# A software-pipelined four-layer attention kernel: another order of the steps on every engine, with other lags and other PSUM banks

## The reference

```python
# L0: causal self-attention, cross-attention on ctx (16 heads of 16), feed-forward
x1 = layernorm(x + mha(x, x, Wq1, Wk1, Wv1, causal=True))
x2 = layernorm(x1 + mha(x1, ctx, Wq2, Wk2, Wv2))
x3 = layernorm(x2 + relu(x2 @ fc1.T + b1) @ fc2.T + b2)
#     in mha: lengths = sum(energy[:, :, 0, :] != 0); columns beyond are masked
# L1: attention of norm(x3) on norm(ctx), a 4-wide gelu MLP, a second attention
att = softmax(normF @ normX.T / 16) @ normX
cross = gelu(att @ w1.T) @ w2.T
nc = layernorm(cross);  x4 = normF + g2 * (cross + g1 * attention(nc, nc, nc))
# L2: x5 = x4 + softmax(x4 @ ctx.T) @ ctx
# L3: 8-head attention on norm(ctx), then a state space scan, then a modulation
x6 = x5 + mha8(layernorm(x5), layernorm(ctx)) @ Wo.T
u = (layernorm(x6) @ W_in.T) @ Bmat
s_t = silu(s_{t-1} @ A.T) + u_t;   out = x6 + s @ Cmat + mod
```

## Time and profile before

| | |
|---|---|
| median of 3 runs | 4112.46 us (4112.36 to 4113.29) |
| profiled execution, span | 4106.6 us (a run's time has 5.9 us more around it) |
| PE busy | 3913.2 us, 95% |
| ACT busy | 3547.9 us, 86% |
| DVE busy | 3349.2 us, 82% |
| POOL busy | 2854.5 us, 70% |

### The profile page before, as it was taken

One profiled execution on the slowest core, in us unless ns is written; L12 is line 12 of the kernel. 1 busy time (PEld: TensorE's weight loads), 2 busy tenths in 40 slices (PEclk: granted clock), 3 DMA queues, 4 the chain that ended last, 5 costly groups with the idle time before them and its releaser, 6 DMA issues. The chain is left out here.

```text
span 4106.6 us, 111739 instructions
## 1 busy us (share of the span) xinstructions
PE 3913.2 (95%) x37177; PEld 3233.6 (79%) x37177; DVE 3349.2 (82%) x9519; ACT 3547.9 (86%) x8460; POOL 2854.5 (70%) x3172
## 2 busy tenths in 40 slices
PE   6899999999999999999999999999999999999859
PEld 5688888888888888888888888888888888887647
DVE  4788888888888888888888888888888888888635
ACT  4799999999998999999899999989999998999635
POOL 2577777777777777777777777777777777777636
PEclk7999999999999999999999999999999999999969
DMA  3001011011101101110110111011011101100038
GB/s 115 22 29 34 20 31 34 20 34 31 34 20 31 34 21 33 31 34 20 31 34 23 31 31 34 20 31 34 23 32 31 34 20 31 34 24 28 18 80 306
DMA packets 121876, 159.94 MB, mean 39 GB/s; under 512 B 12296, under 2 KB 108450, under 8 KB 116642
## 3 DMA queue, kind: packets, MB, share of 16 engines
q1 hardware_dynamic: 116896, 145.39, 11.5%
q10 hardware_dynamic: 4416, 7.41, 0.5%
HBM read 114.86 MB, written 37.75 MB: 37 GB/s over the span
## 5 line engine op out<-in xcount | busy, mean ns | idle before, releaser
L618 PE MATMUL bank<-ident,prob 128*128 128x128 f32 x5120 | 728.8, 277 | 56.9 <-ACT CR L1005 26.9
L938 ACT ACTIVATE probT<-bank 128x512 f32<-128x512 f32 x1280 | 730.6, 593 | 59.6 <-PE bank L618 56.7
L909 ACT ACTIVATE turned<-bank 128x512 f32<-128x512 f32 x896 | 538.7, 601 | 186.9 <-PE bank L554 177.8
L618 PEld LDWEIGHTS bank<-ident,prob 128*128 128x128 f32 x5120 | 590.9, 142 | 138.4 <-issue 48.8
L1138 DVE TENSOR_REDUCE mx<-bank 128x4 f32<-128x512 f32 x768 | 507.9, 682 | 187.3 <-PE bank L589 184.7
L927 ACT ACTIVATE prob<-prob,mx 128x128 f32<-128x128 f32 x2048 | 650.6, 396 | 4.1 <-DVE mx L1127 4.0
L562 PE MATMUL bank<-turned,shared 128*128 128x256 f32 x2560 | 616.4, 384 | 1.2 <-ACT turned L909 1.1
L1444 POOL TENSOR_TENSOR rs_ln<-ve_ln,half 128x2 f32<-128x2 f32 x320 | 227.3, 710 | 446.8 <-DVE ve_ln L1109 446.8
L1149 DVE TENSOR_TENSOR prob<-bank,mx 128x512 f32<-128x512 f32 x768 | 520.7, 685 | 15.3 <-PE bank L618 1.9
L562 PEld LDWEIGHTS bank<-turned,shared 128*128 128x128 f32 x2560 | 469.8, 191 | 69.0 <-issue 12.3
L919 ACT ACTIVATE prob<-prob 128x512 f32<-128x512 f32 x768 | 475.5, 636 | 13.0 <-DVE prob L1149 12.1
(11 more groups left out here) (238 smaller groups left out, 9071.8 us busy)
## 6 DMA issues: line engine op xcount, KB each, us to landing
shared<-in_x SPq DMA_DIRECT2D x128, 256.0 KB, 2.9
CB<-in_ctx SPq DMA_DIRECT2D x64, 256.0 KB, 4.0
CC<-in_ctx SPq DMA_DIRECT2D x64, 256.0 KB, 2.7
mod<-mod_rows SPq DMA_DIRECT2D x64, 256.0 KB, 3.8
residual<-X SPq DMA_DIRECT2D x64, 256.0 KB, 3.1
out<-turned SPq DMA_DIRECT2D x16, 1024.0 KB, 4.8
turned<-residual SPq DMA_DIRECT2D x14, 1024.0 KB, 7.1
u_turned<-us SPq DMA_DIRECT2D x124, 32.0 KB, 2.2
```

Of the source, the lines that this page charges most:

```text
L618: last = nc.tensor.transpose(t[:, h * 128:(h + 1) * 128], src[:, h, :], ident[:])
L909: nc.scalar.activation(dst, banks.of(f"{unit}.{name}")[:, 0:n], ACT.Copy).then_inc(*st["act"].mark(name))
L938: nc.scalar.activation(flat(t), banks.of(f"{att}.turn.{b}{r}")[:, :], ACT.Copy).then_inc(*st["act"].mark(f"probT.{b}{r}"))
```

## The change

No instruction is added, removed or altered. `PROGRAM` has for every engine the same steps in another order, some with another lag; `BANKS` gives most PE steps another bank; `PREPARED` goes from 3 to 2. The greatest lag is still 6. Every line below the table stands 3 lines lower (L618 becomes L621). The lists are long, so one line of each is shown:

```diff
 PROGRAM = {
     "pe": """
-        ctx_att.scores.10@4 mix_att.scores.00@6 pair.cross@5 ctx_att.values.03@4 ctx_att.values.01@4
...
-    ctx_att.turn.10:2 ctx_att.turn.11:0 ctx_att.turn.12:3 ctx_att.turn.13:5 ctx_att.back.1:1 ffn.x2T:6 ffn.fc1:6
...
+    mix_in.k:1 real.ccT:7 ctx_att.out.1:3 ctx_in.x1T:7 ctx_att.back.0:4 mix_att.turn.02:7 ctx_att.back.1:6
...
-PREPARED, MOD_STORED = 3, 6
+PREPARED, MOD_STORED = 2, 6
```

More of the change, by code:

```diff
@@ L146 @@
[L146 to L155, removed]
@@ L156 @@
-        mix_in.v@4 pair.sc1@4 self_att.back.1@2 ctx_att.turn.00@3 mix_in.q@5 ctx_att.turn.02@3 ctx_att.turn.03@3
-        pair.pT1@4 self_in.e0@1 mix_out.u@6 pair.av1@4
+        ctx_att.scores.10@4 mix_att.scores.00@6 pair.cross@5 ctx_att.values.01@4 ctx_att.values.02@4
+        ctx_att.values.00@4 ctx_att.values.03@4 ctx_att.turn.11@4 ctx_att.turn.12@4 ctx_att.turn.10@4
+        ctx_att.turn.13@4 real.ccT@5 mix_in.k@5 ctx_att.values.11@4 ctx_att.values.10@4 ctx_att.values.12@4
+        ctx_att.values.13@4 ctx_in.x1T@3 ctx_att.back.0@4 ctx_att.back.1@4 self_att.scores.03@2
@@ L158 @@
+        self_att.values.10@2 self_att.values.13@2 ctx_att.scores.13@3 ctx_att.scores.12@3 ctx_att.scores.11@3
+        pair.FT@4 mix_in.v@4 real.h5T@5 pair.sc1@4 ctx_att.turn.00@3 mix_in.q@5 self_att.back.1@2 pair.pT1@4
+        ctx_att.turn.03@3 ctx_att.turn.02@3 pair.av1@4 self_in.e0@1 mix_out.u@6
     """,
     "act": """
[L160 to L161 removed]
@@ L162 @@
[L162 to L165, removed]
-        pair.exp2@5 ctx_att.ln2@4 pair.pT2@5 mix_att.probT.03@6 ctx_in.k@3 mix_att.probT.00@6 self_att.exp.00@2
@@ L172 @@
-        real.ln5@5 pair.HCT@4 self_in.v@1
+        ctx_att.exp.00@4 ctx_att.probT.01@4 pair.HCT@5 self_att.outT.1@3 ctx_att.exp.02@4 real.ln5@6 pair.FT@5
+        ctx_att.exp.03@4 mix_in.v@5 real.h5T@6 ctx_att.exp.11@4 pair.exp1@5 ctx_att.exp.12@4 ctx_att.probT.00@4
+        mix_in.q@6 pair.pT1@5 ctx_att.probT.03@4 ctx_att.probT.02@4 pair.gelu@5 self_att.ln1@3 pair.cross@5
+        ctx_att.exp.10@4 ctx_att.exp.13@4 ctx_att.probT.11@4 ctx_att.probT.10@4 ctx_att.probT.12@4
+        mix_att.exp.02@6 ctx_att.probT.13@4 pair.lnN@5 real.ccT@5 ctx_att.outT.0@4 ctx_att.outT.1@4
@@ L215 @@
-    ctx_att.tile.01:4 ctx_att.tile.02:0 ctx_att.tile.03:4 ctx_att.turn.00:3 ctx_att.turn.01:2 ctx_att.turn.02:0
-    ctx_att.turn.03:7 ctx_att.back.0:6 ctx_att.tile.10:2 ctx_att.tile.11:3 ctx_att.tile.12:6 ctx_att.tile.13:5
-    ctx_att.turn.10:2 ctx_att.turn.11:0 ctx_att.turn.12:3 ctx_att.turn.13:5 ctx_att.back.1:1 ffn.x2T:6 ffn.fc1:6
-    ffn.fc2:3 pair.CT:1 pair.FT:0 mix_in.v0:7 mix_in.v1:4 pair.sc1:0 pair.pT1:2 pair.av1:4 pair.cross0:3
-    pair.cross1:0 pair.ncT:1 pair.sc2:1 pair.pT2:6 pair.av:0 real.x4T:4 real.ccT:3 real.screal:6 real.pTreal:7
@@ L223 @@
+    self_att.back.1:4 ctx_att.turn.00:0 mix_in.q:2 ctx_att.turn.02:3 ctx_att.turn.03:5 pair.pT1:1 self_in.e0:0
+    mix_out.u:4 pair.av1:6
 """.split())
```

102 lines of the change are left out of this document (58 added, 44 removed).

## The result

The changed kernel takes 4184.12 us (median of 4 runs, 4173.57 to 4190.68) against 4112.63 for the kernel before (4112.36 to 4113.29 in its 4 runs); the ratio is 1.0174 (95% interval 1.0158 to 1.0190). It is slower, as forecast, but by 71 us where 36 were forecast, and outside the range. The runs of the kernel before lie within 1 us of each other, those of the changed one within 17.

What follows compares the result with a forecast made beforehand. ACT's chain bounds stretch A, PE's own work stretches B and C. Rounds +19 and ramp +17 make 36 us on a 4106.6 span, 4142.6, plus 5.9 around it: 4148 us; range 4095 to 4180, the forecast's own 4125 to 4172.

Steps and rivals of the forecast that it cites:

- Stretch A: Round's part from sc1 to turn.13, as long as ACT's chain: late first norm adds 0.37 us, bounds -0.30 and +0.9.
- the idle 0.30 us may go: In stretch A, ACT's idle 0.30 us ahead of pct's copy may vanish, as PE's pT1 comes sooner.
- Stretch B: Round's part from turn.13 to sc2: x1T waits 0.17 us, sc2 waits 0.33 for ncT's copy; +0.50 us in all.
- Stretch C: Round's part from sc2 to the next sc1: small PE waits go, -0.55 us, bounds -0.6 and +0.5.
- The wait at h5T: In stretch C, PE's 0.20 us wait at step h5T should go, since h5T now stands behind projection v.
- Rival 3: More waits in stretch C, one more late ACT copy costing 0.5 us a round; 4178 us, chance 0.17.
- Per round: Sum of stretches A, B and C: +0.32 us a round, +19 us over 59 full rounds.
- the bounds of B: Stretch B's limits: 0 if ACT runs half a microsecond ahead, +0.9 if self-attention's fourth score tile costs extra.
- The ramp: First rounds, with preparation ahead of round 2: PE waits for biases and round 2's norm; +17 us, bounds +8 and +22.
- The 5.9 us around the span: Time a run was taken to have around its span, added to the forecast span of 4142.6 us.

Runs made afterwards that it cites:

- e15: e6 with back.1 ahead of q in bank 6, the preparation ahead of round 3, and DVE's nz behind the norm's statistics; 4061.36 us, ratio 0.9881.
- e6: e5 with ACT copying ncT ahead of mix_att's turned tile 02, as in the kernel before; 4097.45 us, ratio 0.9968.
- e1: Changed kernel with turn.12, ahead of PE's longest wait, transposing its tile four times, 12 transposes a round more; 4135.42 us, ratio 1.0066.
- e5: Changed kernel with value steps values.00 and values.03 moved on PE from ahead of turn.11 to behind turn.12; 4138.29 us, ratio 1.0070.
- e13: Changed kernel with turn.11 done twice, filling the short wait ahead of turn.12 and leaving the long one behind it; 4133.34 us, ratio 1.0061.
- e3: Kernel before with only the preparation moved, ahead of round 2 and not 3; 4122.51 us, ratio 1.0033.
- e8: e5 with the preparation ahead of round 3 again; 4125.48 us, ratio 1.0038.
- e10: e6 with the preparation ahead of round 3; 4086.47 us, ratio 0.9937, one of four runs left out.

## Why the prediction was right in direction and wrong in size

**Stretch A, forecast +0.37, measured +0.34.** The chain came as worked out. Behind sc1 (2053.20) POOL's rs starts 7.55 us (forecast 7.59) and ACT takes the norm 8.66 (forecast 8.70), where the earlier trace rows had 8.33; DVE's statistics start 6.04 (forecast 6.07).

```profile
2060.75 0.72 POOL L1447 TENSOR_TENSOR rs_ln<-ve_ln,half 128x2 f32<-128x2 f32 x1 [0.37 <-DVE ve_ln L1112]
```
```profile
2061.86 1.09 ACT L991 ACTIVATE X<-Z,nmr_ln,rs_ln 128x256 f32<-128x256 f32 x2 [0.89 <-POOL nmr_ln L1452]
```

The statement "the idle 0.30 us may go" was too small: ACT now waits 0.89 us for the norm, so its own list could end that much sooner, which e15 used in part.

**Stretch B, forecast +0.50, measured +0.41 with the clock up.** sc2 waited 0.24 us (forecast 0.33). x1T did not wait at all (forecast 0.17); instead the value steps start 1.90 us behind the start of k, where k by itself takes 1.73, and what held them these 0.17 isn't shown. **Stretch C, forecast -0.55, measured -0.20.** The wait at h5T went, but x2T got one of 0.33, which e6 shows to be the second half of the late ncT. Rival 3 had foreseen new waits in C, though not by that path.

**Per round, forecast +0.32, measured +0.46 with the clock up (60.31 in e1, 59.85 before); 19 us forecast from it, 18.0 measured** (e1 against the kernel before, first to last cross step). That these two agree is luck: 57 full rounds at +0.46 are 26 us, and the other six, at the two ends, are some 8 us shorter in the new order. The term that was mis-sized is C, of which too much was to come back.

**The step that failed is the clock: the prediction kept it at 1.00, so that PE's idle time costs its own length.** The granted clock is 1.00 in all three stretches of the old order; it priced the new order at 1.00 too ("can lose as much as it makes PE wait"), and its sum has no term for a fall. It asked how long PE would wait in the seam, but not how the waits would lie. What brings them together it doesn't mention: the value steps that stood two ahead of turn.11 and two behind it now all stand ahead, so that only turn.12 is left between the wait for the copy of cross, whose bank it takes (6), and the wait for the exponential. Two of the value steps put back behind turn.12 (e5) or the first wait filled (e13) keep the clock up. The clock fell in 24 of 63 intervals. In the slow round shown, B is 11.78 us long, 1.85 more than the 9.93 before, where the bounds of B ended at +0.9. This is 36.1 us in the profiled execution, and by the medians of e1 and the changed kernel 1.1% or some 44 us. No rival had it. The rest of the slowdown by the medians is some 27 us, 9 less than the 36 forecast, so two errors partly cancel: the miss of 36 us is the clock's 44, less these 9.

**The ramp, forecast +17, measured +11.5 to the first cross step, and 11 to 13 by three experiments.** The single steps came near: PE idle until the preparation, which starts when the last bias lands at 40.90 us (forecast 42.3; its 2 us from the issue to the landing were an estimate, and here it is 1.2, from 39.70), PE back at 59.07 (62.3), round 3 at 93.71 (96) behind a wait for the norm of 8.37 us (8):

```profile
40.90 0.29 DVE L1356 COPY NC<-col_be 128x256 f32<-128x256 f32 x1 [13.41 <-DMA col_k_b<-in_col_k_b]
```
```profile
43.61 1.84 PE L821 MATMUL bank<-col_be,w_q 128*128 128x1 f32 x8 [16.48 <-ACT w_k L1039]
...
59.07 5.07 PE L592 MATMUL bank<-shared,turned 32*128 32x256 f32 x24 [0.56 <-issue]
...
93.71 1.08 PE L557 MATMUL bank<-ident,X 128*128 128x128 f32 x4 [8.37 <-POOL X L1467]
```

Of the 5.5 us too much, 2.3 stand ahead of round 3 (the last bias landed 1.4 sooner, and PE was back 18.2 behind it and not 20.0). The other 3.2 are what comes back: round 3 starts 16.1 us later than in the earlier trace rows, and 4.6 of these are gone by the first cross step, where 1.4 were allowed. POOL's last step of the norm takes 1.26 us here, near the 1.28 that the prediction took, and not the 3.19 of the earlier trace rows, which had the preparation beside it. That it would be short without the preparation beside it was the author's estimate. The runs show it at 1.26 us where the preparation stands ahead of round 2 (the changed kernel, e3, e5, e6) and at 3.19 (the kernel before, e15) or 2.12 (e8, e10) where it stands ahead of round 3. From back.1's end at 84.93 to the end of this step at 93.57 the chain takes 8.6 us, where the forecast took 9.0.

```profile
92.31 1.26 POOL L1467 TENSOR_TENSOR X<-X,row_ln_b 128x512 f32<-128x512 f32 x1
```

**The 5.9 us around the span** are too many. The changed kernel's profiled execution took 4173.57 us with a span of 4171.8, so 1.8 around it, and the experiments' have 1.7 to 1.9; the prediction compared the span of one execution with the median of others. This shifts the forecast by 4 us and decides nothing.

**The range** ended at 4180, at rival 3's 4178. It had no room for a cost that depends on how waits lie.

## What to carry to other kernels

When an order written out by hand is changed, look not only at how much an engine waits but at how its waits lie: on PE, work that stands between two waits may be what keeps the clock up (here 1.00 in every full round of e1, e5 and e13, against 24 slow rounds in the changed kernel), though by the chain it costs and saves nothing. Work that is free (a transpose done again, two steps moved into the gap) can be worth more than a shorter chain. And follow a late copy past its first waiter: the half microsecond of ncT came back 7 us later under another engine's name, and three steps moved in the lists (two value steps on PE in e5, this copy on ACT in e6) turned a kernel 1.7% slower than the one before into one 0.3% faster.
